# Layer two's radial product from bfloat16 parts of the features and the weights

## What is computed

```python
h = jnp.maximum(_layernorm(x, axis=-1), 0.0)
h_e = relu(edge_attr_10 @ W_fc1 / sqrt(10)) * sqrt(2)      # 10 features -> 100
w = h_e @ W_fc2 / sqrt(100)                                # 100 -> 192
y0, y1 = l0[src], l1[src]                                  # linear maps of h, gathered
m = messages(w, y0, y1, edge_attr_4)
out = x + W_si(h) + 0.5 * W_l2(segment_sum(m, dst) / 4)
```

## Time and profile before

| | |
|---|---|
| median of three runs | 2507.64 us |
| lowest, highest | 2506.04, 2508.38 us |
| the profiled execution | 2509.17 us |
| its span in the trace | 2507.4 us |
| mean granted clock of TensorE | 0.986 |
| TensorE, ScalarE, VectorE, POOL busy | 2407.8, 2263.9, 2233.0, 1829.1 us |
| DMA | 333.11 MB, mean 133 GB/s |

### The profile page before, as it was taken

One profiled execution on the slowest core, in us unless ns is written; L12 is line 12 of the kernel. 1 busy time (PEld: TensorE's weight loads), 2 busy tenths in 40 slices (PEclk: granted clock), 3 DMA queues, 4 the chain that ended last, 5 costly groups with the idle time before them and its releaser, 6 DMA issues. The chain is left out here.

```text
span 2507.4 us, 92238 instructions
## 1 busy us (share of the span) xinstructions
PE 2407.8 (96%) x27324; PEld 2322.3 (93%) x27325; DVE 2233.0 (89%) x9898; ACT 2263.9 (90%) x6528; POOL 1829.1 (73%) x2036
## 2 busy tenths in 40 slices
PE   1999999999999999999999999699999999999997
PEld 1999899999999999999999998599999999999997
DVE  6999899999999999999999998288888888888886
ACT  3899899999999999999999998488889888888886
POOL 4888888888888888888888885365555555555551
PEclk9999999999999999999999999599999999999998
DMA  4344444444444444444444443366666566665662
GB/s 140 99 123 126 108 117 126 122 124 123 126 120 125 121 122 125 125 121 126 121 125 122 125 123 91 95 171 161 163 163 161 162 162 162 162 161 158 166 162 77
DMA packets 492136, 333.11 MB, mean 133 GB/s; under 512 B 148236, under 2 KB 475224, under 8 KB 491640
## 3 DMA queue, kind: packets, MB, share of 16 engines
q1 hardware_dynamic: 438693, 241.12, 34.7%
q0 software_dynamic: 48736, 83.76, 14.9%
q10 hardware_dynamic: 4212, 2.34, 0.3%
HBM read 196.32 MB, written 130.68 MB: 130 GB/s over the span
## 5 line engine op out<-in xcount | busy, mean ns | idle before, releaser
L761 POOL DMA_INDIRECT xg<-sources,win x501 | 489.3, 977 | 412.0 <-DVE msg L927 278.0
L761 POOL DMA_INDIRECT xg<-in_x,win x501 | 605.2, 1208 | 148.1 <-issue 125.1
L1269 PE MATMUL out_ps<-w_out,aggT 128*100 128x64 f32 (+2 forms) x6012 | 620.5, 253 | 8.9 <-ACT aggT L1101 6.6
L1269 PEld LDWEIGHTS out_ps<-w_out,aggT 128*100 128x100 f32 x6012 | 592.8, 168 | 11.7 <-ACT aggT L1101 7.4
L1255 PE MATMUL agg_ps<-sel,msg 128*128 128x100 f32 x4512 | 575.7, 278 | 5.4 <-DVE msg L927 4.3
L1255 PEld LDWEIGHTS agg_ps<-sel,msg 128*128 128x128 f32 x4512 | 538.2, 193 | 7.2 <-DVE msg L927 6.7
L1090 ACT ACTIVATE msg<-pw,win 128x64 f32<-128x64 f32 x1503 | 415.9, 351 | 5.6 <-DVE pw L908 5.6
L773 POOL TENSOR_TENSOR rs<-ve,neghalf 128x4 f32<-128x4 f32 x251 | 339.6, 1353 | 20.9
L1101 ACT COPY aggT<-agg_ps 128x600 f32<-128x600 f32 x377 | 248.0, 658 | 34.7 <-PE agg_ps L1336 6.8
L1057 ACT ACTIVATE hn<-xn,nmr,rs 100x192 f32<-100x192 f32 x501 | 244.3, 537 | 33.3 <-DVE nmr L864 33.3
L1118 ACT ACTIVATE h<-xo,nmr,rs 100x192 f32<-100x192 f32 x501 | 247.0, 542 | 2.8 <-DVE nmr L975 2.8
(11 more groups left out here) (159 smaller groups left out, 5693.8 us busy)
## 6 DMA issues: line engine op xcount, KB each, us to landing
ev<-middle SPq DMA_DIRECT2D x250, 250.0 KB
xn<-in_x SPq DMA_DIRECT2D x250, 125.0 KB
out<-xo SPq DMA_DIRECT2D x250, 125.0 KB
middle<-xo SPq DMA_DIRECT2D x244, 125.0 KB
sources<-ev SPq DMA_DIRECT2D x244, 125.0 KB
middle<-ev SPq DMA_DIRECT2D x244, 125.0 KB
ee_sb<-ee_parts SPq DMA_DIRECT2D x501, 18.0 KB
win<-in_edge_rec SPq DMA_DIRECT2D x502, 3.0 KB
```

The source lines that it names most:

```text
L761: pool.indirect_dma_start(out=xg[:, t.slot, j, 0:D], out_offset=None, in_=edge_rows, in_offset=bass.IndirectOffsetOnAxis(ap=win[:, t.place ...
L1269: ins = pe.matmul(rows[0:NT, j, c0:c1], aggT[:, t.half, j, k, :], w[f"out{k}_"][:, :], start=fresh, stop=True, skip_group_check=not fresh)
```

## The change

Layer two's ten features are split into three bfloat16 parts as layer one's are, and the stack is stored three times over, so that each of 90 rows (three copies of three parts of ten features) lies in DRAM and a plain load of 90 rows of 128 bfloat16 values brings a window. The weights are split in setup (VectorE) and nine copies of 10 rows make fc1_parts1. The radial matmul of layer two has 90 rows of bfloat16.

The features are split in layer one's first steps: five chunks of two features, in a ring of four stages. In step s SP issues the load of chunk s, and from step 4 the nine stores of chunk s - 4, after that chunk's last cast and the landing of all stores before; in step 9 it copies the nine weight blocks. ScalarE casts at the start of its step: part 0 of chunk s - 1, part 1 of chunk s - 2, part 2 of chunk s - 3. Part 0 of chunk 4 takes the stage of chunk 0, so that cast also waits until chunk 0's nine stores have landed. VectorE subtracts at the end of its step, after the casts. The setup of ee_sb on ScalarE has half its size, since a slot holds 128 bfloat16 values.

```diff
-    ee_parts = nc.dram_tensor("ee_parts", [PARTS * nf, EP], BF16, kind="Internal").ap()
+    ee_parts = [nc.dram_tensor(f"ee_parts{k}", [PARTS ** (k + 1) * e.shape[0], EP], BF16, kind="Internal").ap() for k, e in enumerate(ee)]
...
+        nf1 = ee[1].shape[0]
+        fc1_parts1 = sb("fc1_parts1", [PARTS * PARTS * nf1, wts["fc1_1"].shape[1]], BF16)
+        w_parts1 = sb("w_parts1", [nf1, PARTS, wts["fc1_1"].shape[1]], BF16)
...
+        found_i = sb("found_i", [P, 2 * TC, ROW], I32)
...
-        ee_sb = sb("ee_sb", [SW, S1, PAIR, 2 * P], BF16)
+        ee_sb = sb("ee_sb", [SW, S1, PAIR, P], BF16)
...
+        second_features = SecondFeatures(nc, sb, sem, dict(locals()))
...
-            act.copy(ee_sb[:, :, :, :].rearrange("p s j (h e) -> p (s j h) e", h=2),
-                     one_rows[0:SW, :].unsqueeze(1).to_broadcast([SW, 2 * PAIR * (RING + 1), P]))
+            act.copy(ee_sb[:, :, :, :].rearrange("p s j e -> p (s j) e"),
+                     one_rows[0:SW, :].unsqueeze(1).to_broadcast([SW, PAIR * (RING + 1), P]))
...
+            for g in range(PARTS):
+                ins = dve.tensor_copy(v["w_parts1"][:, g, :], w["fc1_1"][:, :])
+                if g < PARTS - 1:
+                    link(ins)
+                    link(dve.tensor_tensor(w["fc1_1"][:, :], w["fc1_1"][:, :], v["w_parts1"][:, g, :], ALU.subtract))
+            ins.then_inc(s_wparts, 1)
...
+class SecondFeatures:
+    def __init__(self, nc, sb, sem, v):
+        self.ee, self.parts_out, self.fc1, self.w_parts = v["ee"][1], v["ee_parts"][1], v["fc1_parts1"], v["w_parts1"]
+        self.nf = self.ee.shape[0]
+        self.e = v["found_i"][:, :, :].bitcast(F32).rearrange("p (b f) r -> p b f r", f=FEATS)
+        self.part = sb("part1", [P, STAGES, PARTS, FEATS, ROW], BF16)
+        self.s_ee, self.s_cast, self.s_rest, self.s_parts, self.s_wparts = (v[k] for k in ("s_ee", "s_cast", "s_rest", "s_parts", "s_wparts"))
+        self.cast0, self.rest0, self.parts0 = 2 * PARTS, 2 * (PARTS - 1), 16 * PARTS
+        self.n = self.nf // FEATS
+    def rows(self, c):
+        return slice(c * FEATS, (c + 1) * FEATS)
+    def casts(self, c, g):
+        return self.cast0 + sum(min(max(c + g - q, 0), self.n) for q in range(PARTS)) + sum(1 for q in range(g + 1) if 0 <= c + g - q < self.n)
+    def rests(self, c, g):
+        return self.rest0 + sum(min(max(c + g - q, 0), self.n) for q in range(PARTS - 1)) + sum(1 for q in range(g + 1) if 0 <= c + g - q < self.n)
+    def sync(self, sp, step):
+        if 0 <= step < self.n:
+            c = step
+            sp.wait_ge(self.s_ee, 16 * (c + 1))
+            if c >= STAGES:
+                sp.wait_ge(self.s_cast, self.casts(c - STAGES, PARTS - 1))
+            sp.dma_start(self.e[:, c % STAGES, :, :], self.ee[self.rows(c), :].rearrange("f (p r) -> p f r", p=P)).then_inc(self.s_ee, 16)
+        if 0 <= step - STAGES < self.n:
+            c = step - STAGES
+            sp.wait_ge(self.s_cast, self.casts(c, PARTS - 1))
+            sp.wait_ge(self.s_parts, self.parts0 + 16 * PARTS * PARTS * c)
+            for g in range(PARTS):
+                for i in range(PARTS):
+                    at = (i * PARTS + g) * self.nf + c * FEATS
+                    to = self.parts_out[at:at + FEATS, :].rearrange("f (p r) -> p f r", p=P)
+                    sp.dma_start(to, self.part[:, c % STAGES, g, :, :]).then_inc(self.s_parts, 16)
+        if step == STAGES + self.n:
+            sp.wait_ge(self.s_wparts, 2)
+            for g in range(PARTS):
+                for i in range(PARTS):
+                    at = (g * PARTS + i) * self.nf
+                    sp.dma_start(self.fc1[at:at + self.nf, :], self.w_parts[:, g, :]).then_inc(self.s_parts, 16)
+    def scalar(self, act, step):
+        for g in range(PARTS):
+            c = step - 1 - g
+            if 0 <= c < self.n:
+                if g == 0:
+                    act.wait_ge(self.s_ee, 16 * (c + 2))
+                    if c >= STAGES:
+                        act.wait_ge(self.s_parts, self.parts0 + 16 * PARTS * PARTS * (c - STAGES + 1))
+                else:
+                    act.wait_ge(self.s_rest, self.rests(c, g - 1))
+                act.copy(self.part[:, c % STAGES, g, :, :], self.e[:, c % STAGES, :, :]).then_inc(self.s_cast, 1)
+    def vector(self, dve, step):
+        for g in range(PARTS - 1):
+            c = step - 1 - g
+            if 0 <= c < self.n:
+                dve.wait_ge(self.s_cast, self.casts(c, g))
+                e = self.e[:, c % STAGES, :, :]
+                dve.tensor_tensor(e, e, self.part[:, c % STAGES, g, :, :], ALU.subtract).then_inc(self.s_rest, 1)
+    def stored(self, sp):
+        sp.wait_ge(self.s_parts, self.parts0 + 16 * PARTS * PARTS * (self.n + 1))
...
-    krad = PARTS * nrow + PARTS if first else SW
-    ee_all = ee_sb[:, :, :, 0:P] if first else ee_sb[:, :, :, :].bitcast(F32)
-    fc1 = v["fc1_parts"] if first else w["fc1_"]
+    krad = PARTS * nrow + PARTS if first else nrow
+    fc1 = v["fc1_parts" if first else "fc1_parts1"]
+    second_features = v["second_features"]
...
-                sp.dma_start(ee_all[0:PARTS * nrow if first else nrow, t.slot, j, :], rows).then_inc(win_in[t.slot], 16)
+                sp.dma_start(ee_sb[0:PARTS * nrow if first else nrow, t.slot, j, :], rows).then_inc(win_in[t.slot], 16)
...
+                if first and T(0):
+                    second_features.sync(sp, T(0).n)
...
+                second_features.stored(sp)
+                second = v["ee_parts"][1]
                 for n in range(AHEAD):
                     for j in range(PAIR):
                         begin = sp.snap(regs[n * PAIR + j], min_val=0, max_val=EP - P)
-                        sp.dma_start(ee_sb[:, :, :, :].bitcast(F32)[0:v["ee"][1].shape[0], n, j, :], v["ee"][1][:, bass.ds(begin, P)]).then_inc(v["win_sems"][1][n], 16)
+                        nrow1 = second.shape[0]
+                        sp.dma_start(ee_sb[0:nrow1, n, j, :], second[:, bass.ds(begin, P)]).then_inc(v["win_sems"][1][n], 16)
...
+                if (t := T(0)) and first:
+                    second_features.vector(dve, t.n)
...
+                if (t := T(0)) and first:
+                    second_features.scalar(act, t.n)
...
-                        ins = pe.matmul(hid_ps[0:fc1.shape[1], j, :], fc1[:, :], ee_all[0:krad, t.slot, j, :], start=True, stop=True)
+                        ins = pe.matmul(hid_ps[0:fc1.shape[1], j, :], fc1[:, :], ee_sb[0:krad, t.slot, j, :], start=True, stop=True)
...
-        "fc1_1": below(g1["W_fc1"]), "fc2_1": by_use(g1["W_fc2"]),
+        "fc1_1": g1["W_fc1"], "fc2_1": by_use(g1["W_fc2"]),
```

25 lines of the change are left out of this document (12 added, 13 removed).

## The result

The changed kernel takes 2486.39 us (median of four, 2484.02 to 2489.6), the kernel before in the same series 2508.01 (2506.04 to 2511.44): a ratio of 0.9912, 95% interval 0.99 to 0.9924. It is faster by 22 us where the forecast was 51. The profiled execution took 2486.48 us with a span of 2484.5. A second series gave 2483.77 against 2510.48, 0.9893 (0.9873 to 0.9913).

The account below looks back on a forecast made before the run. TensorE was taken to pace both layers. From the profiled 2509.2, less 66 for layer two, plus 1.4 for setup and 15 for the fill, came 2459.2, taken as 2457 on the median's scale; range 2440 to 2488.

Parts of the forecast that it names:

- The term of 66 us: Layer two's radial matmul in bfloat16: each turn falls from 3.49 to 3.22 us, 0.27 saved over 246 turns.
- ScalarE's wait before the copy of xw: Sign in layer two: ScalarE's only gap in a turn was to fall from 0.35 to below 0.1 us.
- the rival in which it paces layer two: Rival: ScalarE, with 0.09 us to spare, sets layer two's pace at 3.32 us; time 2482, chance 0.12.
- VectorE's wait before line 999: Sign in layer two: VectorE's wait of 0.38 us in a turn was to be little changed.
- the rule on the weight load: Layer two's radial matmul: fast load needs 128 non-float32 weights, so 100 columns load at the plain rate; no row shows it.
- Loads of layer two: 160 more pieces per turn at 25 ns each, 0.25 us more per DMA engine, 74% busy; taken at nothing.
- Setup: Splitting layer two's first weights adds casts and subtractions before layer one: 1.4 us, 2.4 at most.
- about 59: Layer one's first wait: node_h of turn 0 starts near 59 us, ScalarE 6.0 us late for the first features.
- the 15 us forecast for the fill: Layer one's first steps: waits, casts, subtractions and stores, 8 + 2.3 + 0.5 + 1 + 1 + 2 us.
- just hidden: SP in layer one: stores make it 11 to 16 us late, against its lead of 17 on the gathers.
- stores rival: Rival: stores at the setup rate make five steps 30 or 47 us late, beyond the lead; 2479, chance 0.10.
- The sign of it that the prediction asked for: Layer one's fill: the forecast expected no gap near 110 us on SP's window loads.

Follow-up runs that it names:

- no_landing_wait: Changed kernel with five stages of parts instead of four, so neither SP nor ScalarE waits for stores to land; 2707.46 us, 1.0118 of the kernel before.
- best_in_setup_b: Changed kernel with parts stored once and read three times, first four chunks loaded earlier, casts behind copy_hT, weight copies in setup; 2458.99 us, 0.9801 of the kernel before.

## Why the prediction was right in its direction and wrong in its size

**Layer two: right.** The turn of 3.22 us, 0.12 us to the sums and TensorE as the pace came out. The term of 66 us was 62.2: the pace fell by 3.489 - 3.232 = 0.257 us and not by 0.27, a rounding of rows that have 0.01 us each, and 246 x 0.257 is 63. ScalarE's wait before the copy of xw (line 1170) fell from 0.35 to 0.2 and not below 0.1: 35.7 us over 186 turns. The work from that copy to the end of the last spread takes 2005.11 - 2002.06 = 3.05 us now, where I took the 3.13 of before; so ScalarE had more room than I gave it, and the rival in which it paces layer two didn't come. VectorE's wait before line 999 fell from 0.38 to 0.15 us, where I had said that it would change little.

The prediction weighed the rule on the weight load ("TensorE: Matmul & The Clock Gate", in the Trainium skill, section "Weight-path perf modes — Fast Weight Load (FWL) and DoubleRow"). The two layers' radial weight loads in the changed kernel:

```profile
L1309 PEld LDWEIGHTS agg_ps<-ee_sb,fc_parts x501: 96/98/152, 62.5 to 1617.0; 75*128 75x128 bf16 x167
```

```profile
L1311 PEld LDWEIGHTS xw_ps<-ee_sb,fc_parts x501: 125/127/208, 1644.9 to 2472.7; 90*100 90x100 bf16 x167
```

The 100 columns take 127 ns and the 128 columns 98: fewer columns take longer, and the trace agrees with the rule, though it isn't a test of it: rows and columns both differ here. It cost nothing, since from radial to outputs both layers take 1.49 us.

**Loads of layer two: right, and cheaper than taken.** The hardware queue's share between 1700 and 2300 us, before and after:

```profile
q1 hardware_dynamic: 79166, 67.90, 36.8%
```

```profile
q1 hardware_dynamic: 117139, 79.98, 45.5%
```

Per turn that is 0.368 x 9600 / 171.9 = 20.6 us of engine time before and 0.455 x 9600 / 185.6 = 23.5 after, 2.9 us for 160 more pieces: 18 ns each (25 taken), and a DMA share of 0.69 (0.74 forecast). Of the read-modify-write that the Trainium skill states for transfers under 512 B ("DMA: Bandwidth & Descriptors", section "Specifications") this shows no sign: 256 B pieces cost less than half of the gather's 640 B rows. These pieces are reads of DRAM into SBUF, and the measurement decides for them.

**Setup: right.** 1.4 us taken, 1.6 measured.

**The fill up to its casts: right as a sum.** ScalarE's first steps and the landing of the chunks:

```profile
60.32 0.84 ACT L492 CAST part<-found_i 128x784 bf16<-128x784 f32 x1 [33.98 <-DMA found_i<-in_ee]
61.07 0.98 ACT L1150 ACTIVATE hn<-xn,nmr,rs 100x192 f32<-100x192 f32 x2
```

```profile
DMA to landing us min/median/max: 3.4/3.7/4.5
```

node_h of turn 0 starts at 61.07 and not at 52.71, so 8.4 us late where "about 59" had been said. That figure left setup out, which has a term of its own: it moves SP's load to 55.82, 1.3 us later than taken. What is left, 6.9 us against 6.0, is a first landing of 4.5 us (3.5 taken) and a cast of 0.844 us (0.76). A subtraction takes 0.97 and not 0.9. The steps behind it cost less than taken, since the 15 us forecast for the fill came to 13.0 by turn 3, ahead of the stall.

**The stores: the step that failed.** The prediction said: SP's step 8 to 9 us, five times, 11 to 16 us late, against a lead of 17, "just hidden". Three things in it were wrong, in order of weight.

1. *The lead was taken from the wrong item.* I measured SP's lead by its window loads, three turns ahead. In the same queue stand the row stores, which can't be ahead: they go out when the rows are ready. The changed kernel's fill moved everything by 14.6 us, so turn 0's last row store would have gone out at 93.60 + 14.6 = 108.2 (before: 93.60), landed 3.93 later at 112.1, and VectorE came for its slot at 129.29 - 14.96 = 114.3. The slack of that item is some 2 us by this estimate, not 17. It could have been read before the change: there the store of 93.60, taken to land 3.93 later, is done at 97.5, and VectorE writes the slot again at 99.61.

```profile
99.61 0.55 DVE L847 TENSOR_TENSOR xo<-xn,hn 100x384 f32<-100x384 f32 x1
```

 In the changed kernel it went out at 125.36. I listed as gated by the stores only the window loads and the cast of chunk 4, and never asked who waits for a row store.
2. *The issue was taken at 0.40 us.* The part stores' row (duration min/median/max in ns):

```profile
L473 SPq DMA_DIRECT2D ee_parts<-part x45: 403/537/1668, 73.6 to 120.2; - x45
```

 The groups of nine take 4.8 to 6.3 us and not 3.6. The nine small weight copies, which the prediction mentions and never prices, take 6.97 us, 0.77 each: on SP's queue a copy of ten rows holds it longer than a store of 196 KB. From the first group to the fifth (73.63 to 115.87) four steps take 42.2 us, 10.6 each where 8 to 9 were taken, 4.6 over the pace. Why a part store holds the queue for 0.54 us and once for 1.67, where the load of a chunk takes 0.40, isn't shown.
3. *The clock had no term.* The sum and the stores rival price a delay at its length. The stall cost 25.5 us. Of these TensorE is idle for 4.22 + 10.35 + 0.60 = 15.2 in the three stretches above; the other 10 are work at the 1.2 GHz level: from 130 to 152 us TensorE is busy for 21.05 us at a granted clock of 0.50, which by estimate is half of that, 10.5 us, lost.

The rival "the stores outrun the lead" (2479, chance 0.10) had the right mechanism in the wrong place: it let SP wait for landings, while SP waited 1.3 us in all for them (two waits, the longer 0.8) and no_landing_wait stalls for 13.3 us without them, and it had neither the row stores nor the clock. It should have had far more than a tenth. The measured 2486 lies just inside the range only because this rival's bound of 2487 had been taken in, and that its size comes out near is luck. The sign of it that the prediction asked for, a gap near 110 us, is there, though it is on a row store and not on window loads. The fill costs 38.6 us by the table, so by the prediction's own last line ("if the fill costs over 25 us") it is wrong. With the queue mended the time comes near the forecast's 2457, since best_in_setup_b is at 2458.99, but not by the forecast's terms: its turn 30 is 11.6 us late where setup and fill were taken at 16.4, as its chunks are loaded earlier and its casts stand elsewhere, and its layer two takes 839.0 us, as the changed kernel's does.

## What to carry to other kernels

When work is added to a queue, go through everything that stands in this queue and ask of each item how early it can be and who waits for it: the item with the least slack decides, and a store that gives a buffer free is as urgent as a load. Count a queue by its issues, not its bytes: a copy of ten rows held it for 0.77 us here and a store of 196 KB for 0.54 in the median, so one broadcast on reading is cheaper than storing three times, and small copies belong where their queue is idle. And price idle time of TensorE above its length: what followed it here ran at 0.50 of the clock until 152 us.
